# Loads, first probabilities and output splits moved at the borders of a decoder layer, and other fillers in its last waits

## The reference

```python
# 1. gated MLP, width 1376, in which the half of the gates that is smallest in |s| is set to zero
s = silu(x @ w_gate.T);  s = where(the 688 smallest |s| of a row, 0, s)
x = layernorm(x + (s * (x @ w_up.T)) @ w_down.T)
# 2. cross attention, 32 query heads over 8 key heads of 128, rmsnorm on q and k
q = rmsnorm(x @ Wq.T) * q_norm_w;  k = rmsnorm(ctx @ Wk.T) * k_norm_w;  v = ctx @ Wv.T
x = layernorm(x + softmax(q @ k.T / sqrt(128) + mask) @ v @ Wo.T)
# 3. eight experts of rank 16, one per token
logits = x @ route_w.T;  w = one_hot(argmax) * max(logits)
x = layernorm(x + ((w * (x @ A.T)) @ Bw))
```

## Time and profile before

| what | value |
|---|---|
| median of 3 runs | 2726.2 us (2726.06 to 2727.31) |
| the profiled execution | 2725.83 us, of which the span 2724.0 us |
| PE busy | 2702.3 us (99%) |
| PEld busy | 2347.2 us (86%) |
| DVE busy | 2114.2 us (78%) |
| ACT busy | 1450.2 us (53%) |
| POOL busy | 1086.8 us (40%) |
| mean granted TensorE clock | 0.998 |
| chain that ended last | PE 96% |

### The profile page before, as it was taken

How to read it: one execution, slowest core, us unless ns; L and a number is a source line. 1 busy time by engine, 2 the same in 40 slices (tenths; PEclk the granted TensorE clock), 3 DMA queues, 4 the chain that set the end, 5 groups by cost and what they waited for, 6 DMA issues and landing times.

```text
span 2724.0 us, 46900 instructions
## 1 busy us (share of the span) xinstructions
PE 2702.3 (99%) x14633; PEld 2347.2 (86%) x14633; DVE 2114.2 (78%) x3132; ACT 1450.2 (53%) x3153; POOL 1086.8 (40%) x1015
## 2 busy tenths in 40 slices
PE   9999999999999999999999999999999999999999
PEld 8888888888788888888888888888889888888887
DVE  3399999988855567888888888888888888887644
ACT  3233433343424446666666666666666666666421
POOL 0122222223313345555555555555555555554000
PEclk9999999999999999999999999999999999999999
DMA  5253333333343443111121212121111212112532
GB/s 180 91 178 116 108 112 107 115 113 111 93 137 112 127 131 101 54 53 60 57 64 57 64 57 64 57 64 57 50 58 53 64 57 64 57 45 86 189 109 74
DMA packets 258000, 241.64 MB, mean 89 GB/s; under 512 B 12884, under 2 KB 215860, under 8 KB 257944
## 3 DMA queue, kind: packets, MB, share of 16 engines
q1 hardware_dynamic: 257944, 240.94, 28.6%
HBM read 145.05 MB, written 95.85 MB: 88 GB/s over the span
## 4 chain that ended last, share of the span: by engine, by line
PE 96%; DMA 1%; issue 1%; POOL 1%; DVE 1%; ACT 0%; SPq 0%; POOLq 0%; DVEq 0%; ACTq 0%
PE banks L158 26%; PE banks L159 26%; PE banks L160 26%; PE banks L1762 13%; PE banks L383 2%; PE banks L1289 1%; DMA queries<-qT_sb 1%; PE banks L1779 1%; PE banks L1777 1%; PE banks L1012 0%; POOL p_odd L1550 0%; DMA pd_sb<-gated_products 0%; PE banks L2114 0%; DMA raw<-WgT_in 0%; DMA raw<-keys 0%
## 5 line engine op out<-in xcount | busy, mean ns | idle before, releaser
L1718 DVE TENSOR_TENSOR pT_lo<-banks,pT_hi 128x512 fp32r<-128x512 f32 (+1 forms) x832 | 572.9, 689 | 96.3 <-ACT pT_hi L1639 84.1
L1639 ACT CAST pT_hi<-banks 128x512 fp32r<-128x512 f32 x576 | 334.5, 581 | 405.4 <-PE banks L1762 405.4
L620 DVE TENSOR_SCALAR_CACHE_REDUCE flags<-abs_s,cand 128x1376 bf16<-128x1376 f32 x248 | 393.2, 1642 | 1.1
L158 PE MATMUL banks<-k_hi,q_hi 128*128 128x416 f32 (+1 forms) x1024 | 375.3, 366 | 1.2 <-DVE t_min L1674 1.2
L159 PE MATMUL banks<-k_lo,q_hi 128*128 128x416 f32 (+1 forms) x1024 | 353.7, 345 | 0.0
L160 PE MATMUL banks<-k_hi,q_lo 128*128 128x416 f32 (+1 forms) x1024 | 352.0, 344 | 0.0
L158 PE MATMUL banks<-pT_hi,v_hi 128*128 128x512 f32 x768 | 344.1, 448 | 0.2 <-DVE pT_lo L1718 0.2
L158 PE MATMUL banks<-kvw_hi,c_hi 128*128 128x512 f32 x816 | 322.3, 395 | 0.0
L160 PE MATMUL banks<-kvw_hi,c_lo 128*128 128x512 f32 x816 | 318.3, 390 | 0.0
L159 PE MATMUL banks<-kvw_lo,c_hi 128*128 128x512 f32 x816 | 317.6, 389 | 0.0
L1674 DVE CUSTOM_DVE_ANT_0 p_odd<-banks,minus_mask 128x1664 f32<-128x1664 f32 x128 | 242.1, 1891 | 90.8 <-PE banks L160 90.8
(11 more groups left out here) (191 smaller groups left out, 5576.8 us busy)
## 6 DMA issues: line engine op xcount, KB each, us to landing
raw<-keys SPq DMA_DIRECT2D x32, 800.5 KB, 4.5
values<-v_sb SPq DMA_DIRECT2D x50, 512.0 KB, 2.6
keys<-kT_sb SPq DMA_DIRECT2D x50, 512.0 KB, 4.4
raw<-values SPq DMA_DIRECT2D x32, 768.0 KB
queries<-qT_sb SPq DMA_DIRECT2D x64, 256.0 KB, 2.6
raw<-queries SPq DMA_DIRECT2D x32, 512.0 KB, 5.3
attended<-o_sb SPq DMA_DIRECT2D x128, 128.0 KB, 1.9
raw<-attended SPq DMA_DIRECT2D x64, 256.0 KB, 2.9
```

Source lines behind the costliest of these rows:

```text
L158: pe.matmul(out, a_hi, b_hi, start=start, stop=False)
L620: bits.done(dve.tensor_scalar(flags[:, tt % 2], abs_s[:, tt], at[:, tt:tt + 1].bitcast(F32), 0.0, ALU.is_lt, ALU.add, accum_out=out[:, tt: ...
L1639: act.copy(pT_hi[:, m % RING], t_bank(m)).then_inc(pT_hi_act, 1)
L1718: dve.tensor_tensor(pT_lo[r, m % RING], t_bank(m)[r], pT_hi[r, m % RING].bitcast(F32), ALU.subtract).then_inc(pT_lo_done, 1)
```

## The change

Six edits, in the order of the program:

- The third load of gated products (`third_p`) is issued in the last step of the key stage, ahead of that step's two stores, once the first gates have been transposed.
- The second item's keys and queries (`second_kq`) are loaded in step TT + 3 of the last queries, and ACT copies their hi parts in step TT + 7, after the last squares, ahead of the first exponential of the second unit.
- The exponential of tile 3 (`last_exp`) goes ahead of the last squares on ACT.
- The normalization of tile 3 goes from POOL to DVE: a multiplication (128x1601) in step TT + 6, and the copy of 63 columns in step TT + 7, which first waits for POOL's tiles 0 to 2.
- The first two output splits go from (-2, 4) and (-2, 9) to (-3, 10) and (-2, 10), on ACT and POOL.
- A turn of `keep_busy` is a transpose and two products of two columns; the turns are 16, 5, 7 and 4 instead of 28, 5, 12 and 4.

```diff
@@ keys: sync
             if is_tile(i, s + RING):
                 load_c(sp, i, s + RING)
+            if isinstance(i, int) and BODY * i + s == LAST:
+                down.early["third_p"](sp)
             store(i, s)
@@ down: sync
+    def load_p_behind(sp, i, m):
+        sp.wait_ge(hT_done, done(2 * i + m))
+        load_p(sp, 2 * i + m + 2, m % 2)
...
-            if is_tile(i, m + 2):
-                sp.wait_ge(hT_done, done(2 * i + m))
-                load_p(sp, 2 * i + m + 2, m % 2)
+            if is_tile(i, m + 2) and not (isinstance(i, int) and m == 0):
+                load_p_behind(sp, i, m)
@@ queries: sync, scalar
+            if last_trip(i) and s == TT + 3:
+                attention.early["second_kq"](sp)
...
             ahead = upcoming(i, s)
+            if last_trip(i) and s == TT + 5:
+                attention.early["last_exp"](act)
             if ahead is not None:
                 squares(act, i, ahead)
@@ attention: early_gpsimd, early_scalar, early_vector
-        if 4 <= s < 8:
+        if 4 <= s < 7:
             normalize(pool, 0, 0, s - 4)
...
-        if 2 <= s < 6:
+        if 2 <= s < 5:
             exp(act, 0, 0, s - 2)
...
         if s == 7:
+            act.wait_ge(sem("ssq_q"), done(TT * G - 1))
+            for n in range(len(KQ)):
+                split_kq_hi(act, 1, 1, n)
             exp(act, 0, 1, 0)
...
+        if s == 6:
+            last = p_sb[0][:, QT - 1, 0:KV]
+            dve.wait_ge(inv_done, done(QT - 1))
+            dve.tensor_scalar(last, last, p_inv[:, QT - 1:QT], 1.0, ALU.mult, ALU.mult).then_inc(mask_done, 1)
         if s == 7:
+            row = p_sb[0][:, QT - 1]
+            dve.wait_ge(mask_done, 4)
+            dve.wait_ge(p_done, done(2 * (QT - 1) - 1))
+            dve.tensor_copy(row[:, KV:KP], row[:, TAIL:TAIL + KP - KV]).then_inc(p_done, 2)
             subtract_mask(dve, 0, 1, 0)
             split_tail(dve, 0, 0)
@@ attention: gpsimd and scalar; output
-            if last_trip(i) and u >= BODY - 2:
+            if last_trip(i) and u >= BODY - 3:
...
-    EARLY = {(-2, 4): 0, (-2, 9): 1, (-1, 3): 2}
+    EARLY = {(-3, 10): 0, (-2, 10): 1, (-1, 3): 2}
...
             if t == TT - 1:
+                r = (STEPS - 1) % RING
                 for k in range(turns):
                     pe.transpose(psum[:, 7, 0:P], ident, ident)
+                    for h in range(2):
+                        pe.matmul(psum[:, 7, 2 * h:2 * h + 2], o_hi[:, r, h * P:(h + 1) * P], w_hi[h][:, 0, 0:2],
+                                  start=True, stop=True)
...
-                    keep_busy(t, 28)
+                    keep_busy(t, 16)
...
-                    keep_busy(t, 12)
+                    keep_busy(t, 7)
```

More of the change, by code:

```diff
@@ L1075, in down_and_norm @@
     return Stage(sync, gpsimd, scalar, vector, tensor, {
-        "open": open_counts, "first_loads": first_loads, "pad": pad, "split_w": split_w,
+        "open": open_counts, "first_loads": first_loads, "third_p": lambda sp: load_p_behind(sp, 0, 0), "pad": pad, "split_w": split_w,
         "first_gates": lambda act: split_gates_hi(act, 0, 0), "gates": gates, "split_gates": split_gates,
@@ L1490, in last_v, with load_next_kq @@
         load_last_v(sp, 0)
+    def load_next_kq(sp, item):
+        sp.wait_ge(kq_lo, done(len(KQ) * item - 1))
+        load_kq(sp, item)
     def sync(sp):
-        def load_next_kq(item):
-            sp.wait_ge(kq_lo, done(len(KQ) * item - 1))
-            load_kq(sp, item)
         def load_next_v(item):
@@ L1506, in position @@
                 else:
-                    load_next_kq(2 * i + u // 2 + 2)
+                    load_next_kq(sp, 2 * i + u // 2 + 2)
             if last_trip(i) and (u, kt) == (1, 1):
@@ L1523, in position @@
                                  ).then_inc(o_out[u % 2], 16)
-        load_next_kq(1)
         load_next_v(1)
@@ L1665, in scalar @@
             split_p(0, 0, kt)
-        for n in range(len(KQ)):
-            split_kq_hi(act, 1, 1, n)
         schedule(act, position)
@@ L1807, in attention @@
     return Stage(sync, gpsimd, scalar, vector, tensor, {
-        "open": open_counts, "first_loads": first_loads, "last_v": last_v, "gpsimd": early_gpsimd,
+        "open": open_counts, "first_loads": first_loads, "last_v": last_v,
+        "second_kq": lambda sp: load_next_kq(sp, 1), "last_exp": lambda act: exp(act, 0, 0, QT - 1), "gpsimd": early_gpsimd,
         "scalar": early_scalar, "vector": early_vector, "tensor": early_tensor})
```

## The result

| what | before | after |
|---|---|---|
| median of 13 runs of each | 2727.1 us (2725.85 to 2728.54) | 2733.3 us (2726.04 to 2734.94) |
| ratio of the medians | | 1.002, 95% interval 1.0011 to 1.0028 |
| the profiled execution, of which the span | 2725.83, 2724.0 us | 2733.47, 2731.7 us |
| mean granted TensorE clock | 0.998 | 0.994 |

The prediction was 2723.6 us with a range up to 2727.5. The kernel became slower by some 6 us: the wrong side, and outside the range. Eleven of the 13 runs lie between 2731.9 and 2734.9 us, with a mean clock of 0.994 or 0.995; two lie at 2726.0 and 2726.3, with a mean clock of 0.998 and 0.997.

The account below looks back on a forecast made before the run. TensorE was busy 2702.3 of 2724.0 us, leaving idle, half-clock stretches and its work to gain from. Terms -3.0 - 2.6 + 1.2 - 0.35 + 2.2 = -2.55 us gave 2723.6 us as median, range 2719.5 to 2727.5.

Parts of the forecast that it names:

- Down: Third load of gated products in the down stage: issued sooner, it ends TensorE's idle of 2.66 and 0.19 us, -3.0 us.
- Start of attention: Border from queries to attention: direct gain 0.85, waits 1.6, late splits 0.5, less 0.4 for the clock; -2.6 us.
- Now it begins at 1026.7 and ends at 1030.2: Start of attention: DVE's copy, mask subtraction, tail of v and last turned queries keep their 3.5 us, giving -0.85 us.
- stood idle: Start of attention: POOL has no work from 1026.5 to 1032.9, so the second item's three subtractions (6.3 us) fit there.
- The first unit: Attention's first unit: waits of 0.41 and 1.22 us and some 0.5 us of late splits go; it takes 25 to 26 us.
- 0.4 us booked for the clock: Start of attention: the clock falls again and the product runs 0.85 us longer at half clock, 0.4 us given back.
- Output splits: Copies moved to (1, 10) delay o_sb, +1.2 us; moving those at (2, 9) one step later gives -0.35 us.
- Fillers: Last tile's four waits: turns of 0.28 us at full clock overrun the waits they cover, +2.2 us.
- the fillers let the clock fall: Rival, chance 0.09: sparse turns lower the clock in the last waits; up to 2734 us, 2730 if after the first filler.
- four overhangs: Fillers of the last waits: time over their covers, put at 1.0, 0.5, 0.4 and 0.3 us.
- a clock below 1 in the last 15 us: Sign at the end of the kernel, named as showing the forecast wrong.
- x2's transposes beginning about 4.4 us after the last output product: Sign at the first filler, named as showing the forecast right; 3.4 us before the change.

Follow-up runs that it names:

- lock_free: old_fillers with POOL's three subtractions waiting for the end of tile 3 and DVE's tail of v behind the first three pT_lo: 2720.4 us.
- borders_act: old_fillers with the start of attention reordered, the first output split back at (-2, 4), and ACT instead of DVE normalizing tile 3: 2716.7 us.
- old_fillers: Changed kernel with the fillers of before (28, 5, 12 and 4 transposes), everything else as changed: 2723.7 us, ratio to before 0.9986.
- dense_mix: Kernel before with 16, 5, 7 and 4 turns of a transpose and two products of 128 columns as fillers: 2730.7 us, ratio 1.0013.
- new_fillers_alone: Kernel before with only the change's fillers (16, 5, 7 and 4 turns with products of two columns): 2736.7 us, ratio 1.0027.
- long_transposes: Kernel before with fillers of 43, 13, 19 and 11 transposes: 2729.8 us, ratio 1.0012.
- borders_filled: borders_act with 12 and 10 transposes of the identity filling the two waits left at the start of attention: 2716.1 us, ratio to before 0.9962.
- turns_24: Kernel before with 24 turns with products of two columns in the first filler, then 5, 12 and 4 transposes: 2734.5 us, ratio 1.0027.

## Why the prediction was wrong

The prediction came out wrong by two steps of its sum, the start of attention (off by 4.3 us) and the fillers (off by 6.9 us). Either alone would have put the time beyond the range.

- **Down, -3.0.** Right by mechanism and size (-3.2 measured in the traces, confirmed alone).
- **Start of attention, -2.6; measured +1.7.** The step that failed is "Now it begins at 1026.7 and ends at 1030.2". It took DVE's work at its old durations, and POOL's three subtractions as harmless because POOL "stood idle" there. But they begin 0.17 us ahead of DVE's copy and hold it for 1.6 us, then the tail of v for 2.1, and DVE's multiplication held POOL's copy for 0.5. That is 4.2 us, about the whole error of this term. lock_free shows the first two by giving them back, borders_act the third. The multiplication itself, put at up to 2 us, took 1.44. The same effect stood in the trace of before, unread: while POOL normalized tile 3, the first piece of the tail of v took 0.76 us, and its twin right behind it 0.34.

```profile
1027.42 0.76 DVE L1543 SCALAR_TENSOR_TENSOR v_hi<-v_hi,low_rows,raw 128x128 fp32r<-128x128 f32 x1
1028.11 0.34 DVE L1543 SCALAR_TENSOR_TENSOR v_lo<-v_lo,low_rows,raw 128x128 fp32r<-128x128 f32 x1
...
1026.45 1.60 POOL L1550 TENSOR_SCALAR p_even<-p_even,p_inv 128x1601 f32<-128x1601 f32 x1
```

- **The first unit.** Its waits went as forecast. The clock fell again, as forecast, but it was at half for 13.7 us (1023.1 to 1036.8) instead of 6.8 before. The longer idle pieces are one possible cause, and not a shown one: old_fillers has the same instructions and the same waits there, and its mean clock over 1022 to 1037 is 0.77 where the changed kernel has 0.54. So the 0.4 us booked for the clock could not be read from one profile at all.
- **Output splits, +1.2 and -0.35.** The wait for o_sb is right (+1.23). The other gave -0.87: the 0.24 us wait is gone and the one for p_odd is 1.10 after 1.24 us, which is about the forecast; the remaining 0.5 us stand in no wait of the list, and their cause is open.
- **Fillers, +2.2; measured +9.1.** The step that failed is the term that took every turn at full clock. That "the fillers let the clock fall" stood as a rival at 0.09, with 2730 us if it fell after the first filler, which is where it fell. The evidence for the rival was read ("They now stream a transpose for 0.11 of every 0.28 us") and not given weight, because the fillers of before were known to hold; but these streamed all the time, so they said nothing of sparse ones. The rival's own price was good: 6.6 us, where the half clock cost 6.1 (9.1 less the 3.0 of length that dense_mix shows). Its 2730 us was short of 2733.3 because the start of attention failed as well.
- **The length of the fillers.** It was mis-sized too: a turn was put at 0.28 us and takes 0.30. The four overhangs were also rounded down: 16, 5, 7 and 4 turns of 0.28 us are 2.4 us over their covers, not 2.2. By dense_mix the length alone costs 3.0 us.
- The test named for it, "a clock below 1 in the last 15 us", is what the profile shows, and "x2's transposes beginning about 4.4 us after the last output product" came at 4.85.

## What to carry to other kernels

When work moves to an engine that stands idle, look at what runs beside it on DVE and POOL. Here a copy of 63 columns on the path took as long as the rest of a large subtraction beside it, while an instruction that reads PSUM was not held. In a trace this shows as no wait at all: the instruction is too long, and ends when the other engine's ends.

A filler that keeps TensorE busy does not for that reason hold its clock. In this kernel fillers of transposes and products of 128 columns held it in every profile, and rows of 16 or 24 turns with products of two columns lost it in three of four. Fill with full width, and count the instructions to fit the wait. That the old filler held the clock says nothing of a new kind of filler.

Before a change is credited with what the clock did, look at the clock in several runs: the same instructions ran at different clocks here.

## What was not expected of the hardware

- TensorE reads as fully busy (4.86 of 4.86 us) in a row of small products behind which its clock fell (new_fillers_alone), and as fully busy (4.90 of 4.90) in a row with 128-column products behind which it held (dense_mix, on another chip).
- A small product with its own weights costs as much as a wide one in a row: a turn takes 0.30 us with products of 2 columns (4.86 us for 16) and 0.31 with 128 (4.90 us).
- Rows of transposes alone ran at full clock: 43 in a row in 4.86 us (long_transposes), and 22 in the waits at the start of attention (borders_filled). The Trainium skill, "TensorE: Matmul & The Clock Gate", Part 4, says that full clock does not engage for them and that they do not count as busy in the same way; these runs disagree.
- After a fall the clock came back within the tail in the one profile where products and transposes of full width followed (turns_24), and not in the two where sparse turns followed (changed kernel and new_fillers_alone, to the end).
- Under the same instructions and the same waits, the start of attention ran at a mean clock of 0.89 in four profiles and of 0.93 or 0.94 in six.
